# Merging the expert stage of a two-layer transformer kernel into its first attention, with a third stage put in loops

## The reference, cut to what matters

```python
# layer 0
h = layernorm(x); q = ln_head((h @ Wq + bq))            # 16 heads of 16
k, v from ctx[:, :48] by Wk, Wv;  k2, v2 from ctx[:, 48:] by Wkv_dca;  k, k2 = ln_head(...)
x = x + tanh(g) * ((attn(q, k, v) + attn(q, k2, v2)) @ Wo + bo)
h = layernorm(x); probs = softmax(h @ gate_w.T); top 4 of 16 experts, weights normed
x = x + tanh(g) * (sum_e comb[:, e] * swiglu(h, Wg[e], Wu[e], Wd[e])
                   + sigmoid(h @ shared_gate_w) * swiglu(h, sWg, sWu, sWd))
# layer 1
h = layernorm(x); attention over ctx with 16 heads of 128 and 8 key/value heads; x = x + tanh(g) * (...)
h = layernorm(x); a SwiGLU of width 688 whose weights are looked up, w = lut[idx]; x = x + tanh(g) * (...)
```

## Time and profile before

| | us |
|---|---|
| median of 3 runs (490.92 to 492.18) | 491.07 |
| time of the profiled execution | 492.26 |
| its span, first to last instruction | 490.2 |

### The profile page before, as it was taken

The page is one execution under the profiler, slowest core; times in us unless marked ns, Lnnn a source line. Parts: engine busy times, 40 slices in busy tenths (PEclk is TensorE's granted clock), DMA queues, the critical chain, the costliest instruction groups (busy, mean ns, idle before and its releaser), DMA issues. The chain is left out here.

```text
span 490.2 us, 7799 instructions
## 1 busy us (share of the span) xinstructions
PE 413.8 (84%) x2996; PEld 389.4 (79%) x3004; DVE 341.2 (70%) x754; ACT 205.8 (42%) x405; POOL 163.4 (33%) x194
## 2 busy tenths in 40 slices
PE   0637794958666899999999899999999999879996
PEld 0536783857555898999999889999999999869995
DVE  4775759587530576768586488988989978956652
ACT  3263536535222143433433356446455555413331
POOL 3013322142230022222313154464464464334332
PEclk9958596795955599999999999999999999979999
DMA  8103001010010003011020200100100100000000
GB/s 254 40 1 114 16 9 58 0 64 2 28 79 1 0 1 109 1 61 49 15 94 1 67 2 1 57 0 1 57 2 1 46 1 1 1 2 23 23 19 25
DMA packets 6648, 16.25 MB, mean 33 GB/s; under 512 B 1090, under 2 KB 4291, under 8 KB 6100
## 3 DMA queue, kind: packets, MB, share of 16 engines
q1 hardware_dynamic: 6612, 15.75, 9.7%
HBM read 14.70 MB, written 1.05 MB: 32 GB/s over the span
## 5 line engine op out<-in xcount | busy, mean ns | idle before, releaser
L1421 POOL TENSOR_SCALAR work<-work,lut_step,lut 128x344 f32<-128x344 int32 (+1 forms) x60 | 42.1, 712 | 55.3 <-DVE work L1348 53.7
L291 PE MATMUL ps<-wB_hi,workr 128*128 128x256 f32 x224 | 52.6, 298 | 6.0 <-POOL workr L1576 4.5
L291 PE MATMUL ps<-xT_hi,wB_hi 128*128 128x256 f32 x176 | 53.0, 301 | 0.0
L291 PE MATMUL ps<-xT_lo,wB_hi 128*128 128x256 f32 x176 | 51.3, 291 | 0.0
L291 PE MATMUL ps<-xT_hi,wB_lo 128*128 128x256 f32 x176 | 51.2, 291 | 0.0
L291 PE MATMUL ps<-wN_hi,shared_r 128*128 128x256 f32 x256 | 47.5, 280 | 1.3 <-DVE x L1335 1.3
L1014 POOL TENSOR_TENSOR workr<-work,workr 128x256 fp32r<-128x256 f32 (+1 forms) x36 | 22.9, 636 | 71.3 <-ACT workr L897 71.3
L291 PEld LDWEIGHTS ps<-wB_hi,workr 128*128 128x128 f32 x224 | 39.4, 194 | 8.0 <-POOL wB_lo L1426 3.8
L1363 DVE COPY_PREDICATED work<-work 128x1376 f32<-128x1376 int32 (+5 forms) x36 | 41.3, 1146 | 2.3
L291 PEld LDWEIGHTS ps<-wN_hi,shared_r 128*128 128x128 f32 x256 | 40.1, 188 | 1.5 <-DVE shared_r L1325 1.5
L291 PE MATMUL ps<-xT_hi,wM_hi 128*128 128x256 f32 x128 | 36.7, 287 | 3.2 <-ACT work L1189 1.6
(11 more groups left out here) (199 smaller groups left out, 1188.6 us busy)
## 6 DMA issues: line engine op xcount, KB each, us to landing
stage<-in_wC SPq DMA_DIRECT2D x4, 1280.0 KB, 5.4
stage<-in_wB SPq DMA_DIRECT2D x4, 768.0 KB, 4.4
stage<-in_idx SPq DMA_DIRECT2D x4, 536.0 KB, 3.6
stage<-in_wA SPq DMA_DIRECT2D x2, 512.0 KB, 5.6
out<-x SPq DMA_DIRECT2D x4, 256.0 KB, 2.2
x<-in_x SPq DMA_DIRECT2D x1, 768.0 KB, 6.9
ctx_T<-in_ctx_T SPq DMA_DIRECT2D x1, 512.0 KB, 8.0
ctx_n<-in_ctx_n SPq DMA_DIRECT2D x4, 128.0 KB, 2.2
```

Source lines behind the costliest of these rows:

```text
L291: last = nc.tensor.matmul(out, l, r, start=start and i == 0, stop=stop and i == 2)
L1421: nc.gpsimd.tensor_scalar(lev[:, j, 0:n], bits[:, 0, 0:n], lut_step[:, j:j + 1], lut[:, 2 * j:2 * j + 1], ALU.mult, ALU.add).then_inc(*C[" ...
```

## The change

A and B become one stage, written by `pe_AB`, `act_AB`, `dve_AB` and `pool_AB`. Called with g, it does the experts of group g, the second half of A for group g + 1 and the first half of A for group g + 2. It is called for g = -1 (no experts), 0, 1, 2 (no first half) and 3 (experts alone). The pieces of the three are interleaved by hand.

- The experts have two PSUM banks for gate and up products instead of three, and one for the spread weights instead of two; `spread(k)` waits for `weighted(k - 1)` and stands ahead of `gate_up`.
- All 16 joins are made in the last call (g = 3), two after each of the first gate products; their weights go to two buffers in turn.
- The expert weights are loaded at once to a buffer of their own, ahead of `wS`, and split in the call g = -1; PE waits for the last split (`A_prep_lo`) before the call g = 0.
- The norm `xn` moves from DVE to ACT, with an offset made by two small instructions on POOL. The keys are laid out by ACT alone (8 instructions; before 2 on ACT, 6 on DVE).
- Before Ln and Exp the activation table set that has both is loaded by name. Tanh is not in that set.
- `pe_A_first` does only what group 0 needs; the normed input and keys of group 1 move to the call g = -1.
- C's first three groups run in a hardware loop (`Fori`) on all engines, where waits and addresses are computed from the loop's register, and the store of D in one on SP.

The core of the diff, eight columns of indentation and the lines that call `joins` left out:

```diff
+SC = (4, 6)
+KV = (5, 4)
+QK = (4, 5)
+PROBS, VALUES = 6, 6
+A_FRONT, B_FRONT, Q_BANK, TURN_OUT, OUT_A = 4, 1, 6, 6, 7
...
+def front_pool_offset(pool, f):
+    front_pool(pool, f)
+    pool.wait_ge(*front["rstd_ready"].at(f, 1))
+    pool.sem_inc(waited, 1)
+    for t in range(TILES):
+        nc.gpsimd.tensor_scalar(offset[:, t:t + 1], mv[:, t, 0:1], rstd[:, t:t + 1], -1.0, ALU.mult,
+                                ALU.mult).then_inc(*front["offset_ready"].up())
+def front_norm_act(act, f, g):
+    act.wait_ge(*front["offset_ready"].at(f, TILES))
+    if not isinstance(f, int) or f:
+        act.wait_ge(*front["xT_done"].at(f, 0))
+    for t in range(TILES):
+        nc.scalar.activation(xn[:, t, :], x[:, g * TILES + t, :], ACT.Identity, scale=rstd[:, t:t + 1],
+                             bias=offset[:, t:t + 1]).then_inc(*front["xn_ready"].up())
...
+def pe_B_spread(pe, g, k):
+    if k == 0:
+        pe.wait_ge(*Bp["combT_hi"].at(g, 1))
+        pe.wait_ge(*Bp["combT_lo"].at(g, 1))
+    else:
+        pe.wait_ge(*Bp["h3"].at(g, k))
+    nc.tensor.matmul(spread_to, sel[:, k, :], comb_rows, start=True, stop=True).then_inc(*Bp["bc_done"].up())
...
+def front_A(m):
+    return m if isinstance(m, int) and m < 2 else 2 * m - 1
+def front_next(g):
+    return front_B(g + 1) if not isinstance(g, int) or g < GROUPS - 1 else 8
...
+def pe_AB(pe, g, experts, second, first):
+    n, m = g + 1, g + 2
+    last = experts and not second
+    def joins(*js):
+        for j in js if last else ():
+            pe_join(pe, j)
+    if experts:
+        pe_B_logits(pe, g)
+    if second:
+        pe_A_shift(pe, n, 0)
+        pe_A_shift(pe, n, 1)
+    if experts:
+        pe_B_gate_up(pe, g, 0)
+        pe_B_gate_up(pe, g, 1)
+    if first:
+        pe.wait_ge(*A["exp_ready"].at(n, 1))
+        front_pe(pe, front_A(m), A_FRONT)
+        pe_A_kv(pe, m, 0)
+    if experts:
+        pe_B_comb(pe, g)
+        pe_B_gate_up(pe, g, 2)
+    if first:
+        pe.wait_ge(*A["exp_ready"].at(n, TILES))
+        x_split(pe, front_A(m))
+        pe_A_q(pe, m)
+        pe_A_kv(pe, m, 1)
+    if experts:
+        pe_B_spread(pe, g, 0)
+        pe_B_gate_up(pe, g, 3)
+        pe_B_spread(pe, g, 1)
+        pe_B_down(pe, g, 0)
+    if second:
+        if first:
+            pe.wait_ge(*A["q_ready"].at(m, 1))
+        pe_A_probs(pe, n, 0)
+    if experts:
+        pe_B_gate_up(pe, g, 4)
+        pe_B_spread(pe, g, 2)
+        pe_B_down(pe, g, 1)
+    if second:
+        pe_A_probs(pe, n, 1)
+    if experts:
+        pe_B_spread(pe, g, 3)
+        pe_B_gate_up(pe, g, 5)
+        pe_B_down(pe, g, 2)
+    if first:
+        pe_A_turn(pe, m)
+    if second:
+        pe_A_values(pe, n, 0)
+        pe_A_values(pe, n, 1)
+    if experts:
+        pe_B_spread(pe, g, 4)
+        pe_B_gate_up(pe, g, 6)
+        pe_B_down(pe, g, 3)
+    if second:
+        pe_A_turn_out(pe, n)
+    if experts:
+        pe_B_spread(pe, g, 5)
+        pe_B_gate_up(pe, g, 7)
+        pe_B_down(pe, g, 4)
+    if second:
+        pe_A_out(pe, n)
+    if experts:
+        pe_B_spread(pe, g, 6)
+        pe_B_gate_up(pe, g, 8)
+        pe_B_down(pe, g, 5)
+    if first:
+        pe_A_scores(pe, m, 0)
+    if experts:
+        pe_B_spread(pe, g, 7)
+        pe_B_down(pe, g, 6)
+    if first:
+        pe.wait_ge(*A["o_biased"].at(n, 1))
+        pe_A_scores(pe, m, 1)
+    if experts:
+        pe_B_spread(pe, g, 8)
+        pe_B_down(pe, g, 7)
+    front_pe(pe, front_next(g), B_FRONT)
+    if experts:
+        pe_B_down(pe, g, 8)
...
+def act_AB(act, g, experts, second, first):
+    n, m = g + 1, g + 2
+    last = experts and not second
+    def joins(*js):
+        for j in js if last else ():
+            act_join(act, j)
+    if second:
+        act_A_exp(act, n, 0)
+    if first:
+        front_norm_act(act, front_A(m), m)
+    if experts:
+        act_B_router(act, g)
+        act_B_tanh(act, g, 0)
+    if second:
+        act_A_exp(act, n, 1)
+    if experts:
+        act_B_tanh(act, g, 1)
+    if first:
+        front_upper(act, front_A(m), A_FRONT, xTA_hi)
+    if experts:
+        act_B_comb(act, g)
+        act_B_tanh(act, g, 2)
+    else:
+        act_A_prep(act, 0)
+    if experts:
+        act_B_upper(act, g, 0)
+        act_B_tanh(act, g, 3)
+    if second:
+        act_A_probs(act, n, 0)
+    if first:
+        act_A_square(act, m)
+    if experts:
+        act_B_upper(act, g, 1)
+        act_B_tanh(act, g, 4)
+    if first:
+        nc.scalar.preload_act_table_set("natural_log_exp_and_others")
+        act_A_guess(act, m)
+    if second:
+        act_A_probs(act, n, 1)
+    if experts:
+        act_B_upper(act, g, 2)
+        act_B_upper(act, g, 3)
+        act_B_tanh(act, g, 5)
+    if first:
+        act_A_qk(act, m)
+    if second:
+        act_A_an(act, n)
+    if experts:
+        act_B_upper(act, g, 4)
+        act_B_tanh(act, g, 6)
+    if second:
+        act_A_upper(act, n)
+    if first:
+        act_A_k(act, m, (0, 1))
+    if experts:
+        act_B_upper(act, g, 5)
+        act_B_tanh(act, g, 7)
+    if first:
+        act_A_k(act, m, (2, 3))
+    if experts:
+        act_B_upper(act, g, 6)
+        act_B_tanh(act, g, 8)
+    front_norm_act(act, front_next(g), after(g) if experts else 0)
+    if experts:
+        act_B_upper(act, g, 7)
+    else:
+        for i in range(1, GROUPS):
+            act_A_prep(act, i)
+    front_upper(act, front_next(g), B_FRONT)
+    if experts:
+        act_B_upper(act, g, 8)
+    if first and m + 1 < GROUPS:
+        act_A_ctx(act, m + 1)
...
+def dve_AB(dve, g, experts, second, first):
+    n, m = g + 1, g + 2
+    last = experts and not second
+    def joins(*js):
+        for j in js if last else ():
+            dve_join(dve, j)
+    if experts:
+        dve_B_choose(dve, g)
+        dve_B_gated(dve, g, 0)
+        dve_B_route(dve, g)
+    if second:
+        dve_A_sum(dve, n, 0)
+    if experts:
+        dve_B_gated(dve, g, 1)
+        dve_B_comb(dve, g)
+    if first:
+        front_lower(dve, front_A(m), A_FRONT, xTA_hi, xTA_lo)
+        dve_A_kv(dve, m, 0)
+    if experts:
+        dve_B_gated(dve, g, 2)
+        dve_B_weighted(dve, g, 0)
+    if second:
+        dve_A_sum(dve, n, 1)
+    if first:
+        dve_A_q(dve, m)
+        dve_A_kv(dve, m, 1)
+    if experts:
+        dve_B_gated(dve, g, 3)
+        dve_B_weighted(dve, g, 1)
+    if experts:
+        dve_B_gated(dve, g, 4)
+        dve_B_weighted(dve, g, 2)
+    if first:
+        dve_A_var(dve, m)
+    if experts:
+        dve_B_weighted(dve, g, 3)
+        dve_B_gated(dve, g, 5)
+    if first:
+        dve_A_scale(dve, m)
+    if experts:
+        dve_B_weighted(dve, g, 4)
+        dve_B_gated(dve, g, 6)
+    if second:
+        dve_A_lower(dve, n)
+    if first:
+        dve_A_values(dve, m)
+    if experts:
+        dve_B_weighted(dve, g, 5)
+        dve_B_gated(dve, g, 7)
+    if second:
+        dve_A_add(dve, n)
+    front_stats(dve, front_next(g), after(g) if experts else 0)
+    if experts:
+        dve_B_weighted(dve, g, 6)
+        dve_B_gated(dve, g, 8)
+    if first:
+        dve_A_top(dve, m, 0)
+    if experts:
+        dve_B_weighted(dve, g, 7)
+    if first:
+        dve_A_top(dve, m, 1)
+    if experts:
+        dve_B_weighted(dve, g, 8)
+    front_lower(dve, front_next(g), B_FRONT)
+    if first and m + 1 < GROUPS:
+        front_stats(dve, front_A(m + 1), m + 1)
+        dve_A_ctx(dve, m + 1)
+    if experts:
+        dve_B_add(dve, g)
+        dve.wait_ge(*Bp["x_done"].at(g, TILES))
...
+def pool_AB(pool, g, experts, second, first):
+    n, m = g + 1, g + 2
+    if second:
+        pool_A_scale(pool, n, 0)
+    if experts:
+        pool_B_lower(pool, g, 0)
+    else:
+        pool_A_prep(pool, 0)
+    if second:
+        pool_A_scale(pool, n, 1)
+    if experts:
+        for k in range(1, 7):
+            pool_B_lower(pool, g, k)
+    front_pool_offset(pool, front_next(g))
+    if experts:
+        pool_B_lower(pool, g, 7)
+        pool_B_lower(pool, g, 8)
+    else:
+        for i in range(1, GROUPS):
+            pool_A_prep(pool, i)
+    if first and m + 1 < GROUPS:
+        front_pool_offset(pool, front_A(m + 1))
+def sp_AB(sp):
+    sp.wait_ge(setup_dve, 6)
+    sp.dma_start(stage, a["wC"][0:1].rearrange("o p n -> p (o n)")).then_inc(B_prep_in[0], 16)
+    sp.wait_ge(*A["x_done"].at(GROUPS, 0))
     sp.sem_inc(waited, 1)
-    sp.wait_ge(*Bp["join_done"].at(g, 4))
-    sp.sem_inc(waited, 1)
+    for i in range(1, GROUPS):
+        if i > 1:
+            sp.wait_ge(join_done, 4 * i - 4)
+        sp.dma_start((stage, wC_odd)[i % 2],
+                     a["wC"][i:i + 1].rearrange("o p n -> p (o n)")).then_inc(B_prep_in[i % 2], 16)
+    sp.wait_ge(join_done, 12)
...
+    for i in range(GROUPS):
+        sp.dma_start(wB_raw[:, i * GB:(i + 1) * GB],
+                     a["wB"][i:i + 1].rearrange("o p n -> p (o n)")).then_inc(A_prep_in, 16)
     sp.wait_ge(wA_lo_ready, 2)
     sp.dma_start(stage[:, GB:GB + NWS], a["wS"]).then_inc(wS_in, 16)
```

(55 more changed lines are left out.)

826 lines of the change are left out of this document (349 added, 477 removed).

## The result

The changed kernel takes 526.99 us (median of 4 runs, 522.49 to 529.26) against 491.12 for the kernel before: ratio 1.0725, 95% interval 1.0665 to 1.0786. The direction was forecast, the size was not: 503.7 was predicted and 517 was the upper end. Ratios here leave disturbed runs out, so they can differ a little from those of the medians; one per cent is 4.9 us. The profiled execution took 522.49 with a span of 520.7.

What follows compares the result with a forecast made beforehand. A was taken as bound by the engine-to-engine chain, B and C by PE. Span 490.2 - 3.5 (calls 0 to 3) + 17.6 (call -1) - 3.5 (start) + 2.0 (loops) = 502.8; + 2.1 - 1.2 = 503.7 us, range 479 to 517.

Steps and rivals of the forecast that it cites:

- the walk of calls 0 to 3: Merged calls: engine lists followed at full clock, waits added to PE floors; 194.3 us against 197.8, 3.5 won.
- The start: A up to its first Exp: without keys and queries of group 1, 42.3 instead of 45.79, 3.5 us earlier.
- call -1: From A's first Exp to call 0: 46.6 us, PE waiting for POOL's last expert-weight split; 17.6 us longer than before.
- the prediction's addition for half clock: Start of call 0, after PE's long pause: 3.5 us more, giving 57.2 for the call.
- The single waits: PE's waits in calls 0 and 1, 14.7 us per call, the longest inside 3.6 at the turn; 4.6 at the end.
- The idle PE ahead of call 0: End of call -1: PE idle about 10 us for POOL's expert-weight remainders, call 0 starting at 88.9.
- The loops: C's hardware loops: 2 us taken, between nothing and 17 us.
- Rival 2: Merged calls: clock falls to half after the 3.6 us pause at the turn; +14 for two calls, 512; chance 0.10.
- Rival 1: Merged calls: PE finds its work, half of the 49.5 us above the floors does not occur; 480; chance 0.28.
- the floors: Merged calls with PE never waiting: 39.0 for calls 0 and 1, 29.9 call 2, 35.6 call 3; 143.5 us.
- Rival 3: C: the loops cost their upper bound, +15 us, 518; chance 0.08.
- rival 4: Whole kernel: gain and loss cancel, small errors of the walk adding up to -13 +- 1.5; chance 0.07.

Runs made afterwards that it cites:

- run 12: Changed kernel, order of work untouched, with spare products on PE in all its longer pauses: 494.32 us, ratio 1.0056.
- run 5: Changed kernel with ACT's copies and POOL's remainders 1 to 3 of expert weights earlier in call -1: 514.37 us, ratio 1.0439.
- run 1: Changed kernel with 24 spare products on PE in the pause before the turn of calls 0 and 1: 516.31 us, ratio 1.0536.
- run 7: Changed kernel with early splits, values ahead of the turn, and spare products in PE's waits at the ends of calls: 487.67 us, ratio 0.9915.
- run 3: Changed kernel with all loops of C and the queue's loop of D written out again: 525.86 us, ratio 1.0738.
- run 11: Kernel before the change with spare products in all of PE's longer pauses: 472.92 us, ratio 0.9627.
- run 9: Kernel of run 7 with spare products also in the pauses of A's start and call -1: 480.52 us, ratio 0.9793.
- run 4: Changed kernel with PE waiting for single splits, ACT splitting the input before weight copies, POOL making group 2's offset earlier: 523.62 us, ratio 1.0575.

## Why the prediction missed

**What was right.** At full clock the walk of calls 0 to 3 holds to 1.1 us. The start and call -1 were each forecast some 3 us too long. Walked from one point to the next (the 3.5 in brackets is the prediction's addition for half clock):

| | walked | run 12 | after |
|---|---|---|---|
| start of A's first Exp | 42.3 | 39.1 | 41.2 |
| call -1 | 46.6 | 43.5 | 48.8 |
| call 0 | 53.7 (+3.5) | 54.4 | 62.0 |
| call 1 | 53.7 | 52.6 | 58.0 |
| call 2 | 42.5 | 42.5 | 44.2 |
| call 3 and the sum into x | 40.9 | 41.8 | 46.0 |

The single waits are as walked or a little shorter: 1.07 us before the queries (1.6), 1.61 and 1.29 at `down(1)` and `down(2)` (2.0 each), 3.09 at the turn (3.6), 3.3 at the end (4.6). The idle PE ahead of call 0 was 11.3 us (10) and its cause the one named; run 5 confirms it. A table load lasts 1.28 us. From the end of the instruction ahead of it (116.94 + 0.71) to the start of the next (118.97) there are 1.32 us in all. The Trainium skill (ScalarE: Activation LUTs, What ACT_TABLE_LOAD costs) adds a drain of 1.38 us to each; this trace has no room for it, and the measurement decides. The 3.5 for call 0's start was right too: the clock is 0.50 from 89.95 to about 97. The loops cost 0.7 of the 2.0. C's group takes 38.2 with loops, 38.0 without and 37.7 in the kernel before (DVE's additions into x); what the last 0.3 is was not tried.

**The step that failed** is the granted clock: "I followed the four lists ... at full clock", with 3.5 us for the start of call 0 as the only addition. After's span is 17.9 us above the 502.8 forecast, and the rows that exceed their walk are call -1 by 2.2, call 0 by 4.8, call 1 by 4.3, call 2 by 1.7, call 3 by 5.1 and C and D by 0.9, less 1.1 at the start. Run 12 parts this in two. With the pauses filled the span is 492.4, so half clock costs the profiled execution 28.3 us where 3.5 were put down, 24.8 too few. And the forecast without the 3.5, 499.3, is 6.9 above run 12: the walk was too long, most of it in the start and in call -1, which hid a part of the miss. The likely reason, not tried, is that these two were built from rows of before that themselves ran in part at half clock (0.69 from 36 to 42 us, 0.82 in the first row).

The other runs of the changed kernel are 3 to 7 us slower still. No profile of them shows where, but it is in line with one or two more falls at the ends of calls: run 1 has one at the end of call 1 that the profile of the changed kernel has not. With all pauses filled, 12 runs lie within 3.5 us.

**Rival 2 was the mechanism,** with a chance of 0.10 and two faults. It looked only at the turn, although the waits at each call's end, counted at 4.6 us by the same walk, are a pause as well; run 7 shows that filling the ends won as much as filling the turns in run 1 (10.4 against 9.3 us, where the rival had 14 for the turns). And it was ranked low because "PE is busy over 70% of the call": the call's share says nothing of the microseconds behind a pause, as the earlier trace rows already showed with PE busy 8.05 of 9.20 us at 0.50. Rival 1 (PE finds its work) falls: the excess over the floors is there at full clock too (54.4 and 52.6 us in run 12 against 39.0). Rival 3 falls by run 3, and rival 4 by the result.

**Where the 36 us lie.** 21 us are order (run 12 against run 11), of which 8.5 stand ahead of call 0 (DVE reads the first logits at 84.15 in run 12 and at 75.68 in run 9, with the splits early), not the 11 expected. The other 15 are clock: the changed kernel loses 32.9 us to pauses, the kernel before 18.3. The second split comes from differences of timed runs, with intervals of 2 to 3 us on each.

## What to carry to other kernels

Price a pause of TensorE twice: its own length, and the work that runs at half clock behind it. Look for it at every place where the walk finds a wait of some microseconds or several waits close together. Before work is rearranged to fill pauses, put spare products in them in both versions: here they won 3.7% for the old order and showed that the new one, as a whole, is worth less. Preparation moved out of a stage with idle engines needs a new place where its own engine is idle; put just ahead of its use it is on the path.

## What the runs showed of the hardware

- Products that nothing reads can be worth issuing: in the same order, with the same waits, 32.9 us of 527 and 18.3 us of 491 came off when PE's pauses were filled. In the changed kernel the clock fell with the wait of 3.09 us at the turn (1.00 from 116 to 120 us, 0.63 from 120 to 124), which stands right behind the wait of 1.29 us and the six products of `down(2)`. At call 2's end it fell with waits of 1.70 and 0.86 us with little work between them; after the waits of 1.61 and 1.29 us at `down(1)` and `down(2)` it was still 1.00. The same waits do not always have the same outcome (run 1, ends of calls 0 and 1), so a pause of this size is a chance of half clock, not a fixed price.
- Some DVE instructions whose operands all lie in SBUF waited for the end of a POOL instruction: 3.19, 3.49 and 2.31 us for work of 0.2 to 0.3, and at most 0.63 when the POOL instruction was cut to an eighth. One that reads PSUM beside it was not held (`gated(0)`, 0.41 us at 89.96 in run 4). The Trainium skill (SBUF — State Buffer, Who interferes with whom) calls the port pair that the two engines share an exclusive lock, held for the whole instruction; the trace agrees.
- An iteration of the hardware loop cost 0.2 us (0.7 for three, one profiled execution on each side), with five engines looping at once and PE busy 113 of 115 us of it.
